# Local attention: two powers on GpSimd in place of one, and a softmax bias per score bank

## The reference, cut to what matters

```python
h = shift_token(x)                       # second half of the channels from the token before
q, k, v = split(h @ wqkv, 3)             # 8 heads of 64
q = q / clip(norm(q), 1e-12) * q_scale   # l2norm of every head
k = k / clip(norm(k), 1e-12) * k_scale
q, k = rotary_xpos(q, k)                 # rotation and a scale by position
# windows of 128 tokens; each looks at its own keys and at those of the window before
sim = einsum(8 * q, [k_before, k_own])   # 128 x 256 per head, masked: j <= i <= j + 128
attn = softmax(sim)
x = x + (attn @ [v_before, v_own]) @ wo
```

## Time and profile before

| | |
|---|---|
| median of 3 runs | 4188.11 us (4186.72 to 4189.51) |
| the profiled execution's own time | 4188.17 us |
| its span, first to last instruction | 4186.3 us |
| PE busy | 3704.9 us, 89% |
| DVE busy | 2583.9 us, 62% |
| ACT busy | 1609.4 us, 38% |
| POOL busy | 1369.1 us, 33% |
| mean granted TensorE clock | 0.959 |
| first window stage (win0) | from about 2462 to 3016 us |
| second window stage (win1) | from about 3328 to 3874 us |

### The profile page before, as it was taken

One profiled execution on the slowest core, in us unless ns is written; L12 is line 12 of the kernel. 1 busy time (PEld: TensorE's weight loads), 2 busy tenths in 40 slices (PEclk: granted clock), 3 DMA queues, 4 the chain that ended last, 5 costly groups with the idle time before them and its releaser, 6 DMA issues. The chain is left out here.

```text
span 4186.3 us, 60480 instructions
## 1 busy us (share of the span) xinstructions
PE 3704.9 (89%) x21768; PEld 2584.0 (62%) x21768; DVE 2583.9 (62%) x5258; ACT 1609.4 (38%) x3058; POOL 1369.1 (33%) x1500
## 2 busy tenths in 40 slices
PE   6888878887899999999989978888799888888799
PEld 3666666666444888888875645555555455555444
DVE  4889889888565555555544446666534366666333
ACT  5766666664000222222211225555411255555111
POOL 4777777876000000000002223333211133333111
PEclk8999999999899999999999989999999999999899
DMA  1000000000201000000002111111111111110210
GB/s 37 1 11 11 11 3 9 11 6 11 91 30 46 9 11 12 11 11 11 13 15 93 65 60 31 31 31 33 55 48 50 44 31 31 31 31 27 72 60 31
DMA packets 153364, 128.70 MB, mean 31 GB/s; under 512 B 24280, under 2 KB 150728, under 8 KB 152840
## 3 DMA queue, kind: packets, MB, share of 16 engines
q1 hardware_dynamic: 153096, 125.15, 9.6%
HBM read 87.34 MB, written 37.77 MB: 30 GB/s over the span
## 5 line engine op out<-in xcount | busy, mean ns | idle before, releaser
L841 PE MATMUL ssm_pu<-ident,ssm_ub 128*128 128x128 f32 x2048 | 325.8, 292 | 79.3 <-POOL ssm_ub L333 47.4
L841 PEld LDWEIGHTS ssm_pu<-ident,ssm_ub 128*128 128x128 f32 x2048 | 257.3, 150 | 218.6 <-issue 88.2
L333 POOL TENSOR_SCALAR ssm_ub<-ssm_uT,ssm_bcT 128x512 f32<-128x512 f32 x512 | 355.2, 712 | 94.5 <-ACT ssm_uT L391 60.1
L347 POOL TENSOR_TENSOR ssm_acc<-ssm_acc,ssm_weighted 128x512 f32<-128x512 f32 x256 | 327.9, 1288 | 144.2 <-ACT ssm_weighted L473 143.9
L853 PE MATMUL ssm_pt<-ident,ssm_state 128*128 128x128 f32 x2048 | 288.3, 285 | 82.4 <-DVE ssm_acc L641 58.6
L2243 PE MATMUL win_pa<-win_w_wqkv,win_hT 128*128 128x512 f32 x768 | 359.7, 605 | 1.5 <-ACT win_hT L2039 1.1
L2014 POOL TENSOR_TENSOR win_rotated<-win_straight,win_turned 128x512 f32<-128x512 f32 x128 | 163.1, 1275 | 552.0 <-DVE win_turned L2128 552.0
L631 DVE TENSOR_TENSOR_SCAN ssm_state<-ssm_da,ssm_carry,ssm_pu 128x512 f32<-128x512 f32 x256 | 312.3, 1261 | 22.1 <-PE ssm_pu L841 16.8
L2059 ACT ACTIVATE win_probs<-win_sc,win_nbias,win_rn 128x256 f32<-128x256 f32 x512 | 282.0, 560 | 97.3 <-DVE win_nbias L2157 97.3
L1836 PE MATMUL glu_up<-glu_hT,glu_w_w 128*128 128x512 f32 x640 | 293.2, 615 | 25.9 <-DVE glu_act L1784 22.4
L631 DVE TENSOR_TENSOR_SCAN ssm_state<-ssm_da,ssm_pu 128x512 f32<-128x512 f32 x256 | 296.7, 1200 | 24.2 <-PE ssm_pu L841 16.0
(11 more groups left out here) (241 smaller groups left out, 7258.4 us busy)
## 6 DMA issues: line engine op xcount, KB each, us to landing
win_raw<-in_tables SPq DMA_DIRECT2D x64, 128.0 KB, 2.2
a<-win_y SPq DMA_DIRECT2D x64, 128.0 KB, 1.7
glu_xs<-a SPq DMA_DIRECT2D x32, 256.0 KB, 3.2
glu_x<-a SPq DMA_DIRECT2D x16, 512.0 KB, 5.2
ssm_x<-in_L_attn_x SPq DMA_DIRECT2D x8, 512.0 KB, 3.9
x<-ssm_out SPq DMA_DIRECT2D x16, 256.0 KB, 2.2
moe_x<-x SPq DMA_DIRECT2D x8, 512.0 KB, 3.9
x<-moe_y SPq DMA_DIRECT2D x8, 512.0 KB, 2.9
```

The lines of the kernel that those rows point to most:

```text
L333: nc.gpsimd.tensor_scalar(ub[:, i % 2, t, :], uT[:, k % 2, t, :], bcT[:, k % 2, t, n:n + 1], 1.0, ALU.mult, ALU.mult).then_inc(ub_ready.se ...
L347: nc.gpsimd.tensor_tensor(acc[:, k % 2, t, :], acc[:, k % 2, t, :], weighted[:, j, :], ALU.add)\
L841: last = nc.tensor.transpose(pu[c][:, t * P:(t + 1) * P], ub[:, i % 2, t, c * P:(c + 1) * P], ident)
```

## The change

The power of the 16 sums of squares is taken in two instructions of 8 each, the keys' (j = 1) first, then the queries' (j = 0). `rn_ready` counts two steps for each turn, and `unit_keys` waits for the first of them alone. `square_sums`, which overwrites `ss`, waits for the floor instruction (`kept_ready`) and no longer for the power.

In `maxima`, the bias of the four heads in one instruction becomes one instruction for each score bank, with two heads each. The bias of bank 0 stands after the first mask-and-maximum of bank 1, that of bank 1 after its second. `nb_ready` counts four steps for each turn and `exps` waits for its own bank's. Nothing else is changed.

```diff
--- before.py
+++ after.py
@@ -1931,14 +1931,14 @@
         table_ready = s.counter("table_ready")
         tp_ready, hT_ready = s.counter("tp_ready"), s.counter("hT_ready", credit=1)
         proj_ready, sq_ready = s.counter("proj_ready", per=3), s.counter("sq_ready", per=2, credit=1)
-        ss_steps, rn_ready = s.counter("ss_steps", per=2, credit=1), s.counter("rn_ready", credit=1)
+        ss_steps, rn_ready = s.counter("ss_steps", per=2, credit=1), s.counter("rn_ready", per=2, credit=1)
         kept_ready = s.counter("kept_ready")
         rot_ready, sum_ready = s.counter("rot_ready", per=2, credit=1), s.counter("sum_ready", per=2, credit=1)
         k_unit_ready = s.counter("k_unit_ready")
         v_ready = s.counter("v_ready", credit=1)
         qkt_ready = s.counter("qkt_ready", per=2, credit=1)
         qT_ready, kT_ready = s.counter("qT_ready"), s.counter("kT_ready")
-        st_ready, max_ready, nb_ready = s.counter("st_ready", per=4), s.counter("max_ready", per=4), s.counter("nb_ready", per=2)
+        st_ready, max_ready, nb_ready = s.counter("st_ready", per=4), s.counter("max_ready", per=4), s.counter("nb_ready", per=4)
         exp_ready = s.counter("exp_ready", per=8, credit=1)
         pt_ready = s.counter("pt_ready", per=4)
         p_even, p_odd = s.counter("p_even", per=2), s.counter("p_odd", per=2)
@@ -2015,7 +2015,8 @@
                 pool.wait_ge(ss_steps.sem, ss_steps.at(turn.i))
                 nc.gpsimd.tensor_scalar(ss_kept[:, :, :], ss[:, :, :], 1e-24, None, ALU.max).then_inc(kept_ready.sem, 1)
                 pool.wait_ge(kept_ready.sem, kept_ready.at(turn.i))
-                nc.gpsimd.tensor_tensor(rn[:, turn.side, :, :], ss_kept[:, :, :], minus_half[:, :, :], ALU.pow).then_inc(rn_ready.sem, 1)
+                for j in (1, 0):
+                    nc.gpsimd.tensor_tensor(rn[:, turn.side, j, :], ss_kept[:, j, :], minus_half[:, j, :], ALU.pow).then_inc(rn_ready.sem, 1)
 
             def body(turn, before, more, more2):
                 if more:
@@ -2053,7 +2054,7 @@
                                                 ACT.Copy).then_inc(v_ready.sem, 1)
 
             def exps(turn, g, j):
-                act.wait_ge(nb_ready.sem, nb_ready.at(turn.i, g + 1))
+                act.wait_ge(nb_ready.sem, nb_ready.at(turn.i, 2 * g + j + 1))
                 for r in range(2):
                     head = 4 * g + 2 * r + j
                     nc.scalar.activation(
@@ -2132,12 +2133,12 @@
 
             def square_sums(turn, j):
                 dve.wait_ge(sq_ready.sem, sq_ready.at(turn.i, j + 1))
-                dve.wait_ge(rn_ready.sem, rn_ready.at(turn.i - 1))
+                dve.wait_ge(kept_ready.sem, kept_ready.at(turn.i - 1))
                 nc.vector.tensor_reduce(ss[:, j, :], squares[:, j, :].rearrange("p (h d) -> p h d", d=DH),
                                         AX.X, ALU.add).then_inc(ss_steps.sem, 1)
 
             def unit_keys(turn):
-                dve.wait_ge(rn_ready.sem, rn_ready.at(turn.i))
+                dve.wait_ge(rn_ready.sem, rn_ready.at(turn.i, 1))
                 dve.wait_ge(sum_ready.sem, sum_ready.at(turn.i))
                 nc.vector.tensor_tensor(
                     k_unit[:, :].rearrange("p (h d) -> p h d", d=DH),
@@ -2146,17 +2147,26 @@
 
             def maxima(turn, g):
                 mask = masks[:, 2 if turn.side else 0 if turn.i % (L // P) == 0 else 1, :]
-                for j in range(2):
-                    dve.wait_ge(st_ready.sem, st_ready.at(turn.i, 2 * g + j + 1))
-                    for r in range(2):
-                        last = nc.vector.tensor_tensor_reduce(sc[j][:, r, :], sc[j][:, r, :], mask, 1.0, -3e38,
-                                                              ALU.add, ALU.max, highest[:, g, j, r:r + 1])
-                    last.then_inc(max_ready.sem, 1)
+
+                def highest_of(j, r):
+                    return nc.vector.tensor_tensor_reduce(sc[j][:, r, :], sc[j][:, r, :], mask, 1.0, -3e38,
+                                                          ALU.add, ALU.max, highest[:, g, j, r:r + 1])
+
+                def bias_of(j):
+                    dve.wait_ge(max_ready.sem, max_ready.at(turn.i, 2 * g + j + 1))
+                    nc.vector.scalar_tensor_tensor(
+                        nbias[:, g, j, :], highest[:, g, j, :], -1.0,
+                        rn[:, turn.side, 0, 4 * g + j:4 * g + 4:2], ALU.mult, ALU.mult).then_inc(nb_ready.sem, 1)
+
+                dve.wait_ge(st_ready.sem, st_ready.at(turn.i, 2 * g + 1))
+                highest_of(0, 0)
+                highest_of(0, 1).then_inc(max_ready.sem, 1)
+                dve.wait_ge(st_ready.sem, st_ready.at(turn.i, 2 * g + 2))
+                highest_of(1, 0)
                 dve.wait_ge(rn_ready.sem, rn_ready.at(turn.i))
-                dve.wait_ge(max_ready.sem, max_ready.at(turn.i, 2 * g + 2))
-                nc.vector.scalar_tensor_tensor(
-                    nbias[:, g, :, :], highest[:, g, :, :], -1.0,
-                    rn[:, turn.side, 0, 4 * g:4 * g + 4].rearrange("p (r j) -> p j r", j=2), ALU.mult, ALU.mult).then_inc(nb_ready.sem, 1)
+                bias_of(0)
+                highest_of(1, 1).then_inc(max_ready.sem, 1)
+                bias_of(1)
 
             def columns(turn, g):
                 dve.wait_ge(pt_ready.sem, pt_ready.at(turn.i, 2 * g + 2))
```

## The result

The changed kernel takes 4064.44 us (median of 4 runs, 4062.84 to 4065.74), the kernel before 4187.41 beside it (4186.48 to 4189.51). The ratio is 0.9705, with a 95% interval from 0.9689 to 0.9722. The profiled execution took 4062.84 us, the shortest of the four, and has a span of 4060.9 us against 4186.3, so 125.4 us went there.

What follows compares the result with a forecast made beforehand. The prediction took one closed loop of 17.09 us a turn as the bound. Power -1.28, multiply -0.41 and bias +0.12 made -1.57 us a turn, 100.7 in all, from 4188.17 to 4087 us, range 4066 to 4178.

Steps and rivals of the forecast that it cites:

- The loop and the power: GpSimd's power in the turn's loop: waiting for the keys' 8 elements, 1.65 us in place of 2.93, saves 1.28.
- The closed loop: Window turn of 17.09 us: square sums, power, unit keys, copy, keys' transposes, weighted sums and next scores follow one another.
- The bias's second step: Window turn, g = 1: earlier exponentials bring the second scores forward up to 0.38 us, but its maxima gain nothing.
- The bias's price: VectorE in g = 1: one more small bias instruction delays the square sums by 0.12 us, bounds 0 and 0.30.
- The unit keys' multiply: VectorE, beside the queries' power: held for 0.10 us only, it costs 0.79 rather than 1.205, 0.41 less.
- a rival that it does: Queries' power holds the unit keys' multiply to its end: 2.13 us, 4174 us in all, chance 0.18.
- the sum: Whole kernel: 1.57 us less in each of 62 turns and 1.69 in each of two first windows, together 100.7.
- What is late next: TensorE's own order: keys' transposes could start at 2622.11 us, the loop puts them at 2622.15; TensorE just not the bound.
- The range: Whole kernel: 4066 to 4178 us, the low end with multiply at 0.69, bias at nothing and power 0.12 cheaper.
- cover: TensorE in the window turn: the earlier scores bring its own work forward, counted as no gain in time.
- The signs that were named: Changed profile: powers 1.65 us, multiply 0.7 to 0.9, keys' transposes' wait 0.0 to 0.4, turn within 15.1 to 16.9.

Runs made afterwards that it cites:

- e1_power: The kernel before with the two powers, keys' first, and the new waits, but the old single bias: 4076.14 us, ratio to before 0.9738.
- e4_one_bias_late: The changed kernel with a bias for each bank only for g = 0 and one instruction for all four heads in g = 1: 4057.60 us.
- e8_wide_power: The changed kernel with the queries' power taken over 32 elements, the same 8 numbers four times: 4068.59 us in one run.
- e3_table: The changed kernel with GpSimd's table multiply moved between the keys' power and the queries': 4096.42 us, ratio to before 0.9789.
- e5_keys_first: The changed kernel with one bias for g = 1, and the keys' squares summed first with a floor of their own: 4048.93 us, ratio 0.9669.
- e7_both: The changed kernel, but the unit keys wait for both powers: 4218.79 us, ratio to before 1.0081.

## Why the prediction was right in kind and too small in size

**The loop and the power: right.** The closed loop was the right account. Its steps before and after add up to the turn, and each experiment moved the turn by what the loop or TensorE's order said. The power of 8 was put at 1.65 and is 1.651; the term was 1.28 and is 1.26.

**The bias's second step: the step that failed.** The prediction said that the maxima of g = 1 start "when VectorE ends the rotation that began at 2613.78 with the keys' projection, so they gain nothing". In the trace of before they start 1.47 us after that rotation. In the changed kernel they start 1.27 after it (2612.51 to 2613.78), and so they do in every run whose second score group starts 5.09 to 5.12 behind the first; in e1_power, where it is 5.54 as before, they start 1.48 after. So VectorE was waiting for the scores, by 0.2 us. The hint was there to be read: where VectorE stands idle for the scores of g = 0, the maxima start 1.17 after them (2608.49 behind 2607.32 in the changed kernel, and the same in before), and those of g = 1 started 1.13 after theirs (2615.25 behind 2614.12). I read the small gap ahead of them as the spacing of instructions, because no idle time was printed there. This is 0.21 us a turn, 12 us in the 58 middle turns, about half of what was missing (23 us by the medians, 25 by the two profiled spans). The bias's price, 0.12, was right, though made up otherwise: a hold of 0.2 by GpSimd's rotation sum, less a little spacing; in e4_one_bias_late the bias stands behind that sum and takes 0.16.

**The unit keys' multiply: right mechanism, too small.** The forecast was that the queries' power does not hold it for long, against a rival that it does. I took a hold of 0.10 and a gain of 0.41; there is no hold, and the gain is 0.53: 0.12 more, 7 us in 58 turns. The row that the argument stood on, an addition begun 0.17 before a power's end, was too thin for the bound, and e8_wide_power gives what it lacked. By the rule quoted from the Trainium skill (page "SBUF — State Buffer"; for two SBUF inputs it stands in the section "SBUF: two separate sides"), that the instruction which starts first has the shared pair for its whole length, the multiply would have taken 2.13. The rule holds here for GpSimd's streaming instructions (e3_table, 1.22 beside the table) and not for a power, neither of 1.65 nor of 5.43 us; the measurement decides.

**Edges.** By the two spans 125.4 us went where the sum had 100.7. Of these 25 us the 58 middle turns are 17 (1.87 each in place of 1.57). The first and last turns gave 7.5 us where the sum had 6.3, the ends of the stages 2.7 and the longer turns 1.7 where it had nothing, and 1.6 lie elsewhere: 7 us more than the sum together. The stretches ahead of the first scores gave the 3.4 of the sum.

**What is late next: nearly right.** TensorE was named with 15.1 us of work to a turn, and "just not the bound". In the changed kernel the loop still rules, by 0.25 at the keys' transposes (0.75 behind the queries', where 0.50 is possible); in e1_power and e5_keys_first TensorE rules.

**The range.** Its lower end let the multiply, the bias and the power be at their best and left the scores' step at zero, for which I had worked out a gain elsewhere and called it cover. A term put at nothing had no bound in the range. The signs that were named could not catch it: the powers (1.651), the multiply (0.69), the transposes' wait (0.1 or none) and the turn (15.22, inside 15.1 to 16.9) all came out as said, to a hundredth.

## What to carry to other kernels

When a chain through three engines sets the turn, cut the instruction in it to what the next one needs and put that part first; the rest then runs under cover (1.26 us of 2.93 here), and the split without the order costs time (e7_both). A small wait that the timeline does not print as idle may still be a wait: compare the gap with the same pair of instructions elsewhere before it is put at zero (0.21 us a turn here). And look at what GpSimd runs just beside a VectorE instruction with two SBUF inputs, since moving one short streaming multiply away was worth 0.53 us a turn.

## What the runs showed of the hardware that I had not expected

- GpSimd's power does not keep VectorE's two-input instructions out: 0.692 us for 512 elements beside a power of 8, 0.733 beside one of 32 that took 5.43, against 1.21 beside a multiply of 256 elements that takes 0.73 (after, e8_wide_power, e3_table).
- The other way round a power of 8 takes longer when it starts while such a VectorE instruction runs: 2.09 us (e3_table) and 1.98 (e5_keys_first), where the multiply began first, against 1.64 to 1.67.
- Powers on GpSimd cost about 0.37 us and 0.16 for each element and lane (an estimate from the first three): 1.008 for 4, 1.651 for 8, 2.929 for 16; 5.43 for 32 lies 0.06 under that line.
- In e7_both, with TensorE idle for 2.2 us in nearly every turn, its granted clock fell to the lower level (1.2 GHz) for a few us about every seventh turn. In the profiled execution the longer turns cost 16 us.
